# A head's softmax sums multiplied out in four quarters of the queries, on 32 output partitions each

## What is computed

```python
# x (16, 512, 1024) f32, mask = cond_2048 (16, 1024) of 0 and 1, Wq, Wo (512, 512)
xt = transpose(x, (0, 2, 1))                       # 16 x 1024 tokens x 512
qh = (xt @ Wq.T).reshape(B, T, 8, 64)              # 8 heads of 64; keys and values are the queries
scores = scale * einsum('bhqd,bhkd->bhqk', qh, qh)
logits = (scores * cmask + (1 - cmask) * NEG) * rmask
attn = softmax(logits)                             # over the keys
out = x + transpose(einsum('bhqk,bhkd->bhqd', attn, qh) @ Wo.T)
```

## Time and profile before

| | before |
|---|---|
| median of 3 runs | 1617.94 us (1615.75 to 1622.37) |
| profiled execution: time, span | 1618.75 us, 1617.0 us |
| mean granted PE clock over the span | 0.979 |
| busy, share of the span | PE 1537.4 us (95%), PEld 1222.1 (76%), DVE 1187.3 (73%), ACT 850.0 (53%), POOL 1339.3 (83%) |

### The profile page before, as it was taken

One profiled execution on the slowest core, in us unless ns is written; L12 is line 12 of the kernel. 1 busy time (PEld: TensorE's weight loads), 2 busy tenths in 40 slices (PEclk: granted clock), 3 DMA queues, 4 the chain that ended last, 5 costly groups with the idle time before them and its releaser, 6 DMA issues. The chain is left out here.

```text
span 1617.0 us, 33177 instructions
## 1 busy us (share of the span) xinstructions
PE 1537.4 (95%) x10956; PEld 1222.1 (76%) x10956; DVE 1187.3 (73%) x2659; ACT 850.0 (53%) x2055; POOL 1339.3 (83%) x1069
## 2 busy tenths in 40 slices
PE   6798999999999999999999999999999999999995
PEld 3666778787877778787777778777877777777863
DVE  5356787877878787777878778787877778787773
ACT  2145655565555556555555555555555555555450
POOL 5558989889898989889898988989898897987771
PEclk9689999999999999999999999999999999999997
DMA  3433454444445445354444535444544544453410
GB/s 115 104 83 94 111 129 119 113 122 106 122 106 127 122 110 130 98 130 102 123 122 111 136 93 131 101 121 122 123 127 99 129 106 117 115 131 90 108 50 30
DMA packets 93810, 179.09 MB, mean 111 GB/s; under 512 B 24704, under 2 KB 24832, under 8 KB 93632
## 3 DMA queue, kind: packets, MB, share of 16 engines
q1 hardware_dynamic: 64448, 109.71, 29.2%
q0 software_dynamic: 29184, 67.17, 14.5%
HBM read 36.77 MB, written 33.55 MB: 43 GB/s over the span
## 5 line engine op out<-in xcount | busy, mean ns | idle before, releaser
L870 DVE TENSOR_REDUCE small_mxp<-max_scores 108x1 f32<-108x270 f32 x1280 | 547.9, 436 | 269.0 <-PE max_scores L1069 209.3
L751 ACT ACTIVATE small_Pt<-scores,small_kbias 108x270 f32<-108x270 f32 x1280 | 553.0, 484 | 351.7 <-PE scores L1088 335.6
L596 POOL TENSOR_TENSOR small_Pacc<-small_Pacc,small_Pt 108x540 f32<-108x540 f32 x384 | 517.7, 1348 | 116.4 <-ACT small_Pt L751 109.7
L1069 PE MATMUL max_scores<-small_ops 128*108 128x270 f32 x1280 | 412.8, 329 | 17.8 <-DVE small_mxp L870 16.7
L1100 PE MATMUL ctx_psum<-small_Pt,small_V 108*64 108x270 f32 x2560 | 314.7, 393 | 0.0
L900 DVE RECIPROCAL small_rsum<-small_rsum 128x67 f32<-128x67 f32 (+1 forms) x512 | 240.7, 532 | 74.9 <-ACT small_rsum L698 59.5
L1069 PEld LDWEIGHTS max_scores<-small_ops 128*108 128x108 f32 x1280 | 219.1, 173 | 87.6 <-issue 43.4
L1085 PE MATMUL scores<-small_ops 128*108 128x270 f32 x1280 | 270.4, 290 | 4.7 <-ACT small_Pt L751 4.0
L1100 PEld LDWEIGHTS ctx_psum<-small_Pt,small_V 108*64 108x64 f32 x2560 | 185.1, 137 | 107.3 <-issue 0.5
L1088 PE MATMUL scores<-small_ops 128*108 128x270 f32 x1280 | 263.6, 287 | 0.0
L1085 PEld LDWEIGHTS scores<-small_ops 128*108 128x108 f32 x1280 | 191.8, 173 | 25.3 <-issue 9.4
(11 more groups left out here) (108 smaller groups left out, 2356.6 us busy)
## 6 DMA issues: line engine op xcount, KB each, us to landing
small_ops<-small_H SPq DMA_DIRECT2D x512, 135.0 KB
small_ops<-small_L SPq DMA_DIRECT2D x256, 135.0 KB
small_ops<-small_mrow SPq DMA_DIRECT2D x128, 2.1 KB
small_xg<-x_rows,small_idx POOLq DMA_INDIRECT x80, 4.1
small_xtail<-x_rows,small_idx POOLq DMA_INDIRECT x80, 3.7
out_rows<-small_xtail,small_idx POOLq DMA_INDIRECT x80, 3.1
out_rows<-small_xg,small_idx POOLq DMA_INDIRECT x80, 3.3
wq_sb<-wq SPq DMA_DIRECT2D x1, 1024.0 KB, 5.5
```

What stands on the lines that cost most here:

```text
L596: nc.gpsimd.tensor_tensor(acc, other, t["Pt"][:R, p0], ALU.add).then_inc(pacc_step, 1)
L751: nc.scalar.activation(t["Pt"][:R, (NT * s + k) % f.NP, half, :], ST[(2 * (NT * h + k) + half) % 3][:R, 0:H], ACT.Exp, bias=t["kbias"][:R, ...
L870: nc.vector.tensor_reduce(t["mxp"][:R, h % 2, m // 2, m % 2:m % 2 + 1], MX[m % 2][:R, 0:H], AX.X, ALU.max).then_inc(mx_red, 1)
L1069: nc.tensor.matmul(MX[m % 2][:R, 0:H], ops[:, OPA, tile_cols(m // 2)], ops[:, OPB, half_cols(m % 2)], start=True, stop=True).then_inc(mx_r ...
```

## The change

`rsum` shrinks from 270 to HS = 135 columns. The job `L` of a split form becomes four matmuls, one for each quarter of the queries (135 columns), on 32 output partitions each. `keep_sums` and the reciprocals run over 135 columns instead of 270, the latter in two pieces instead of four, at the same place. `scale` now has to bring a quarter's 32 partitions of reciprocals to the 64 partitions of the head's values: four multiplications of 32 partitions by 135 columns for each half in the place of one of 64 by 270, written out as two quarters by two blocks of 32 partitions.

```diff
@@ -49,7 +49,7 @@
 MT_AT = 1
 CTX_HIGH_AT = {(0, 4): 3, (4, 1): 0, (4, 4): 1, (6, 4): 2}
 CTX_LOW_AT = {(1, 1, 0): 3, (4, 4, 0): 0, (5, 1, 0): 1, (7, 1, 0): 2}
-RECIPROCAL_AT = [(2, 1), (2, 1), (2, 1), (2, 1)]
+RECIPROCAL_AT = [(2, 1), (2, 1)]
 SCALE_AT = [(3, 0), (3, 1)]
 MASKED_AT = [(0, 0), (0, 1)]
 
@@ -84,6 +84,9 @@
 
 
         self.split = split
+
+        self.HS = self.H // 2 if split else self.H
+        self.NRECIP = 2 if split else 4
 
         self.values_at = {2: [(1, k) for k in range(NT)]} if split else \
             {k: [(0, k - 1) if k else (1, NT - 1)] for k in range(NT)}
@@ -405,7 +408,7 @@
             keep("Pacc", [P, f.NA, 2, f.H], F32)
             if not f.split:
                 keep("ctxraw", [P, f.H], F32)
-            keep("rsum", [P, f.H], F32)
+            keep("rsum", [P, f.HS], F32)
             keep("w", [P, 2, D], F32)
             keep("xbarT", [P, KD], F32)
             keep("xsum", [P, D], F32)
@@ -695,7 +698,7 @@
 
                     act.wait_ge(l_ready, s + 1)
                     at_least(act, ctx_done, s)
-                    nc.scalar.activation(t["rsum"][:], MB[bank][:, 0:H], ACT.Identity,
+                    nc.scalar.activation(t["rsum"][:], MB[bank][:, 0:f.HS], ACT.Identity,
                                          bias=tiny[:, 0:1]).then_inc(rsum_done, 1)
 
                 def max_row(h, b, s, bank):
@@ -896,7 +899,7 @@
                 def reciprocal(s, quarter):
 
                     dve.wait_ge(rsum_done, s + 1)
-                    cols = slice(H * quarter // 4, H * (quarter + 1) // 4)
+                    cols = slice(f.HS * quarter // f.NRECIP, f.HS * (quarter + 1) // f.NRECIP)
                     nc.vector.reciprocal(t["rsum"][:, cols], t["rsum"][:, cols]).then_inc(recip_step, 1)
 
                 def ctx_low(b, pair):
@@ -908,7 +911,7 @@
                 def scale(s, h, b, par, half):
 
                     if half == 0:
-                        dve.wait_ge(recip_step, 4 * (s + 1))
+                        dve.wait_ge(recip_step, f.NRECIP * (s + 1))
                         if f.split:
                             dve.wait_ge(pv_done, NT * (s + 1))
                         else:
@@ -918,9 +921,16 @@
                         elif h == 0:
                             at_least(dve, out_ready, NT * b)
                     r0, pr, cols = DK * half, DK * (h % 2), slice(half * H, half * H + H)
-                    last = nc.vector.tensor_tensor(
-                        t["ctx"][pr:pr + DK, h // 2 % 2, cols] if f.split else t["ctxT"][pr:pr + DK, h // 2, cols],
-                        t["rsum"][r0:r0 + DK, :], CT[r0:r0 + DK, 0:H] if f.split else t["ctxraw"][r0:r0 + DK, :], ALU.mult)
+                    if f.split:
+                        for quarter in range(2):
+                            for block in range(0, DK, 32):
+                                q0, at = 32 * (2 * half + quarter), quarter * f.HS
+                                last = nc.vector.tensor_tensor(
+                                    t["ctx"][pr + block:pr + block + 32, h // 2 % 2, half * H + at:half * H + at + f.HS],
+                                    t["rsum"][q0:q0 + 32, :], CT[r0 + block:r0 + block + 32, at:at + f.HS], ALU.mult)
+                    else:
+                        last = nc.vector.tensor_tensor(t["ctxT"][pr:pr + DK, h // 2, cols], t["rsum"][r0:r0 + DK, :],
+                                                       t["ctxraw"][r0:r0 + DK, :], ALU.mult)
                     if half == 1:
                         last.then_inc(ctx_done, 1)
 
@@ -997,7 +1007,7 @@
                     for name, arg, bank, before in jobs:
                         job(name, arg, bank, B, B % 2, HEADS * B - 1)
                         if name == "L":
-                            for quarter in range(4):
+                            for quarter in range(f.NRECIP):
                                 alone("reciprocal", quarter, B, B % 2, -1)
                             for half in range(2):
                                 alone("scale", half, B, B % 2, -1)
@@ -1191,9 +1201,17 @@
                     elif name == "L":
 
                         pe.wait_ge(pacc_step, (NT - 1) * (s + 1))
-                        for half in range(2):
-                            last = nc.tensor.matmul(mb[DK * half:DK * half + DK, 0:H], ones64[:R, :],
-                                                    t["Pacc"][:R, arg % HEADS % f.NA, half, :], start=True, stop=True)
+                        acc = t["Pacc"][:R, arg % HEADS % f.NA]
+                        if f.split:
+                            for quarter in range(4):
+                                at = quarter % 2 * f.HS
+                                last = nc.tensor.matmul(mb[32 * quarter:32 * quarter + 32, 0:f.HS], ones64[:R, 0:32],
+                                                        acc[:, quarter // 2, at:at + f.HS], start=True, stop=True,
+                                                        tile_position=(0, 32 * quarter))
+                        else:
+                            for half in range(2):
+                                last = nc.tensor.matmul(mb[DK * half:DK * half + DK, 0:H], ones64[:R, :], acc[:, half, :],
+                                                        start=True, stop=True)
                         last.then_inc(l_ready, 1)
                     elif name == "out":
                         if chunks[0] == 0:
```

## The result

| | before | after |
|---|---|---|
| median | 1617.4 us (4 runs, 1615.75 to 1622.37) | 1705.8 us (4 runs, 1704.94 to 1708.27) |
| ratio to before | | 1.055 (95% interval 1.0533 to 1.0567) |
| profiled execution: time, span | 1618.75, 1617.0 us | 1705.56, 1703.7 us |
| busy: PE, DVE, POOL | 95%, 73%, 83% | 91%, 74%, 78% |
| waits of PE `max_scores` for reductions | 16.7 us, 28 times | 89.1 us, 134 times |

The change makes the kernel 88 us slower, as forecast (1705). One statement ahead of the prediction has to be put right first: a batch takes 93.7 us, not 98.3, so the window of the earlier trace rows holds a little more than a batch; in a window of one batch, 700.0 to 793.7 us, PE is busy for 92.28 us and idle for 1.4 instead of 1.6. The sums per batch were built from heads and multiplied by the number of batches, and stand.

A forecast was written before the change was run, and what follows sets the result against it. PE was taken as the bound, in a short loop with DVE's reductions. 1618.75 us plus 95 for PE's waits minus 9 for PE's faster sums gave 1705 us; range 1628 to 1734, with 1685 to 1725 given 0.58.

The forecast's parts named there:

- L with what it does to the values: On PE, four quarters side by side plus a change of form: 0.44 us against 0.51, 9 us saved in the run.
- The price for the change from 32 to 64 partitions: On PE between L and the values: 0.09 us, taken from 64 to full width, plus 0.05 for a first load.
- ACT and reciprocals: Two reciprocals fewer take 0.9 us a head, 120 us in all, off DVE where it then idles: worth nothing.
- DVE's price for a piece: In `scale` on DVE: 0.295 us a piece, 0.325 apart with each change of partitions; each half grows by 0.83 us.
- What it does to PE: Later reductions make PE's `max_scores` wait: 6.15 us a batch over eight heads, times 15.5 batches, 95 us.
- the walk: Following DVE's reductions and multiplications head by head to PE's next `max_scores`: 0 to 1.3 us late a head.
- The signs that were named: Expected profile: PE's waits near 100 us, PE busy about 92%, DVE's busy time up some 50 us, pieces 0.32 us apart.
- Rival 1: On DVE: pieces overlap, 0.205 us each, 1628 us; with cases up to 1685, chance 0.18.
- the slip in the length of a half: In the overlapping-pieces walk on DVE: four pieces taken as four times the spacing, 0.82 us, growth some 0.4.
- Rivals 2 and 3: 2: reduction 8's delay absorbed, 1592 to 1610 us, chance 0.12. 3: PE's quarters not side by side, 1734 or 1790, 0.07.

The follow-up runs named there:

- e4: Kernel before the change with two of the four reciprocals left out; 1618.66 us, ratio 0.9995.
- e8: Kernel before the change with only half 1's multiplication cut in four pieces of 32 x 135, half 0 left whole; 1674.3 us, ratio 1.0337.
- e10: Kernel before the change with only `ctx_low` of pair 0 moved from behind reduction 8 to ahead of reduction 6 of head 4; 1644.81 us, ratio 1.0162.
- e12: Changed kernel with `ctx_low` of pair 0 one step later, behind reduction 1 of head 5; 1705.42 us, ratio 1.0549.
- e3: Kernel before the change, each multiplication cut in two of 64 x 135, each repeated into a spare tensor, all from the same starting partitions; 1658.59 us, ratio 1.0244.
- e1: Changed kernel without its eight small multiplications: one of 64 x 270 for each half, reading the 135 columns of reciprocals twice; 1610.98 us, ratio 0.9949.
- e2: Kernel before the change with each 64 x 270 multiplication cut in four of 32 x 135; 1737.39 us, ratio 1.0731.
- e9: Changed kernel with `ctx_low` of pair 0 moved ahead of reduction 6 of head 4; 1705.04 us, ratio 1.0537.
- e11: Changed kernel with pieces spread ahead of reductions 6 to 9 and `ctx_low` of pair 0 ahead of reduction 6 of head 4; 1651.67 us, ratio 1.0195.

## Why the prediction was right

**PE.** Forecast 0.44 us for L with what it does to the values, measured 0.42 (0.36, and 0.06 longer values): 0.09 saved instead of 0.07. The price for the change from 32 to 64 partitions, taken from the change from 64 to full width, fits: 0.36 is 2 x 0.114 + 0.05 + 0.09. Without it L would have taken 0.28 to 0.30 us, by the same terms. By the rule of the Trainium skill ("TensorEngine Tiling (Array Packing)", Key Properties) a change of tiling mode drains the array. The extra 0.06 to 0.09 us agrees with that; no run here has the change of form without it, so that it is this drain is not shown.

**ACT and reciprocals.** Nothing, confirmed by e4 (111 us of DVE's busy time gone, not the 120 of the estimate); the expected longer idle time ahead of reduction 6 is there (1.28 us against 0.17).

**DVE's price for a piece.** Forecast 0.295 us and 0.325 apart, measured 0.291 and 0.30 to 0.31. The gap after the end of the one before is 0.01 to 0.02 instead of 0.03. A half grows by 0.75 instead of 0.83 us.

**What it does to PE.** Forecast 5.6 us a batch with PE's gain taken off, measured 5.3 by heads. Heads 0, 1, 2 and 6 are each 0.05 to 0.15 below the walk, as the cheaper pieces make them; heads 3 and 4 are 0.27 and 0.41 below it. In head 5 the walk gave 1.23 and 1.96 came. That step was mis-sized: the walk left every other instruction of DVE as long as it was, and the delay itself made one of them 1.0 us longer (e8, e10). e12 adds that moving this one away gives back only 0.27 us, for it then crowds the next reductions. 15.5 x 5.3 is 82 us of the 87 by which the span grew. The other 5 us lie outside of the medians: the first batch loses 8.6 us instead of 5.3, the batch with the drop of the clock 6.8, and 1.8 us come in behind the start of the last head with `max_scores`. For the first batch the lower clock (0.85 against 0.90 over 60 to 200 us, so 42 us at 1.2 GHz against 28) is a candidate and was not tested. The prediction had no term for the clock, and none for POOL, of which it said only that it is not late. So the total fits to 1 us partly because errors of both signs cancel. The mechanism is shown; the agreement to 1 us is luck.

**The signs that were named.** PE's waits at 89 us ("near 100"), PE busy 91% (92%), pieces as said. DVE's busy time grew by 72 us instead of some 50: 13 us of it are longer `ctx_low` (65.0 us against 52.4 in all), and the forecast took 137 us off for the reciprocals, a sum of durations that overlap, where the busy time falls by 111.

**The rivals.** Rival 1 (overlapping pieces) is ruled out by the spacing, and its own number was 18 us too low, as e3 shows (the slip in the length of a half, and head 1): it would have been near 1655 - 9 = 1646. Rivals 2 and 3 are ruled out by e1 and by PE's rows.

## What to carry to other kernels

An instruction cut into four costs more than a quarter each: 0.29 us for 32 x 135 against 0.43 for 64 x 270, four times the elements. Each step to another group of partitions takes another 0.1 us of overlap away. Look for the place and not for the busy share: 111 us of DVE work taken from a covered place gave nothing, while 0.75 us more between two reductions on which PE waits came back in full in every head without slack. A layout that saves PE 0.09 us is dear if it has to be undone on the engine in PE's shortest loop; undoing it in four places instead of two got back 59 of 88 us, and no place was found that gives back all.

## What the runs showed of the hardware that was not expected

A DVE instruction with two SBUF operands takes 0.71 us alone and 1.65 to 1.86 when it starts just behind a POOL addition of 1.35 us: it ends 0.58 us after that addition, wherever in it it started (408 of 441 cases; in the others the addition is the one that waits). It stretches POOL's next one as well: 1.75 us in the kernel after (row at 1049.81), against 1.28 for the same instruction of the same batch in e12, where the collision is gone:

```profile
1046.21 1.28 POOL L587 TENSOR_TENSOR small_xsum<-small_xsum,small_xtail 108x512 f32<-108x512 f32 x1
```

Moving one such instruction costs 25 us in the whole run (e10) without any change in the work, so a small shift upstream can have a price that no sum of durations shows.

A stop of PE seems to cost more than its own length; the link is one of place, and no run tests it by itself. Between 200 and 1500 us the granted clock fell to 0.50 (1.2 GHz) only beside PE's longest stop of a batch, 1.45 us (the kernel after once, e2 and e12 four times each, e9 twice) or 1.96 to 2.16 us (e10 and e11, five times each), at about 1.5 us a time. It did not fall there in any kernel whose steady stops were shorter, and not in e8 either, with 1.42 us.
